# A language model tower on one core: stage ends without the drain of GpSimd's transfer queue

## The reference, cut to what matters

```
h = embedding(x) * 16                        # table of 50000 rows in three parts, a projection each
h = h + four_blocks(layernorm(h))            # per block: q, k, v, a linear attention, gelu, two layer norms, FF 1024
h = h + shared_and_routed_ffn(layernorm(h))  # 8 experts, weights truncated to whole numbers
h = h + attention(layernorm(h))              # 16 heads of 16
h = h + experts64(layernorm(h))              # 64 experts, top 8 of 4 of 8 groups, 256 slots each, and a shared expert
```

## Time and profile before

| | us |
|---|---|
| median of 3 runs | 1364.64 |
| span of the profiled execution, first to last instruction | 1361.2 |
| median less span | 3.4 |
| stage 1 (to 55.5) | 55.5 |
| stage 2 (55.5 to 826.8) | 771.3 |
| stage 3 (826.8 to 925.4) | 98.6 |
| stage 4 (925.4 to 1205.0) | 279.6 |
| stage 5 (1205.0 to 1361.2) | 156.2 |

### The profile page before, as it was taken

The page is one execution under the profiler, slowest core; times in us unless marked ns, Lnnn a source line. Parts: engine busy times, 40 slices in busy tenths (PEclk is TensorE's granted clock), DMA queues, the critical chain, the costliest instruction groups (busy, mean ns, idle before and its releaser), DMA issues. The chain is left out here.

```text
span 1361.2 us, 15556 instructions
## 1 busy us (share of the span) xinstructions
PE 1145.9 (84%) x4506; PEld 634.1 (47%) x4506; DVE 688.7 (51%) x1935; ACT 602.7 (44%) x995; POOL 302.8 (22%) x314
## 2 busy tenths in 40 slices
PE   5649999999999999999999885665987877868872
PEld 4424444444444444444444433441554445446661
DVE  2245645664556455644564513636878854522221
ACT  3335554555455544554455222351674553014431
POOL 5000100000000000000000001107001765427774
PEclk9769999999999999999999896885998878889996
DMA  3200110221012200112011102055743216138997
GB/s 92 95 0 0 43 66 8 74 74 42 4 61 81 73 19 23 66 50 96 9 43 43 43 0 79 1 116 116 123 71 62 102 54 208 63 113 170 181 232 125
DMA packets 56755, 99.57 MB, mean 73 GB/s; under 512 B 10327, under 2 KB 37555, under 8 KB 56440
## 3 DMA queue, kind: packets, MB, share of 16 engines
q1 hardware_dynamic: 37544, 55.94, 15.4%
q0 software_dynamic: 19152, 42.92, 12.2%
HBM read 55.33 MB, written 53.00 MB: 80 GB/s over the span
## 5 line engine op out<-in xcount | busy, mean ns | idle before, releaser
L418 PE MATMUL b_ring<-b_H,b_w 128*128 128x512 f32 x512 | 224.8, 592 | 0.0
L418 PE MATMUL b_ring<-b_X1T,b_w 128*128 128x512 f32 x512 | 223.5, 595 | 0.0
L612 POOL TENSOR_TENSOR b_rstd<-b_veps,b_mhalf 128x4 f32<-128x4 f32 x32 | 32.6, 1019 | 707.0 <-DVE b_veps L69 707.0
L418 PE MATMUL b_ring<-XT,b_wqkv 128*128 128x512 f32 x384 | 174.8, 599 | 7.0 <-DMA b_wqkv<-in_wqkv 7.0
L418 PEld LDWEIGHTS b_ring<-b_X1T,b_w 128*128 128x128 f32 x512 | 96.5, 191 | 116.3 <-issue 109.5
L418 PEld LDWEIGHTS b_ring<-b_H,b_w 128*128 128x128 f32 x512 | 96.1, 190 | 115.2 <-issue 115.2
L568 ACT ACTIVATE b_H<-b_ring,b_cur 128x512 f32<-128x512 f32 x128 | 88.0, 687 | 76.9 <-PE b_ring L418 69.8
L418 PEld LDWEIGHTS b_ring<-XT,b_wqkv 128*128 128x128 f32 x384 | 71.5, 193 | 85.8 <-issue 78.1
L669 DVE RECIPROCAL b_rec<-b_den 128x1024 f32<-128x1024 f32 x16 | 104.9, 6553 | 0.6
L1773 DVE TENSOR_REDUCE a_nmax<-a_pA 128x2 f32<-128x512 f32 x128 | 84.8, 687 | 31.7 <-PE a_pA L1469 29.6
L543 ACT ACTIVATE b_ffo<-b_ring,b_cur 128x512 f32<-128x512 f32 x32 | 22.0, 687 | 170.1 <-PE b_ring L418 170.1
(11 more groups left out here) (309 smaller groups left out, 1799.9 us busy)
## 6 DMA issues: line engine op xcount, KB each, us to landing
xe<-b_nil POOLq DMA_DIRECT2D x16, 1284.0 KB, 5.3
x_rows<-xe SPq DMA_DIRECT2D x32, 321.0 KB, 3.9
b_w<-in_w SPq DMA_DIRECT2D x8, 1024.0 KB, 5.2
x_wt<-in_wexp SPq DMA_DIRECT2D x16, 384.0 KB, 4.4
b_wqkv<-in_wqkv SPq DMA_DIRECT2D x4, 768.0 KB, 4.6
qparts<-f_part SPq DMA_DIRECT2D x8, 384.0 KB, 5.0
right<-qparts SPq DMA_DIRECT2D x16, 192.0 KB, 4.8
left<-qparts SPq DMA_DIRECT2D x16, 192.0 KB, 5.1
```

The lines of the kernel that those rows point to most:

```text
L418: last = pe.matmul(bank[:, :], lhsT(k), rhs(k), start=(k == 0), stop=(k == n_k - 1))
L612: pool.tensor_tensor(rstd[:, :], veps[:, :], mhalf[:, :], ALU.pow).then_inc(s_rs, 1)
```

## The change

In each of the five functions one argument is added:

```
-        block = ctx.enter_context(nc.Block())
+        block = ctx.enter_context(nc.Block(no_gpsimd_drain=True))
```

## The result

| | before | after |
|---|---|---|
| first measurement, median | 1364.83 us (4 runs) | 1355.24 us (1353.56 to 1357.98, 4 runs) |
| ratio, first measurement | | 0.9935, 95% interval 0.9918 to 0.9952 |
| ratio, second to fourth | | 0.9954 (0.9936 to 0.9971), 0.9957 (0.9941 to 0.9972), 0.9956 (0.9943 to 0.9970) |
| all runs of the four measurements, median | 1364.26 us (63 runs) | 1357.83 us (1353.56 to 1359.96, 23 runs) |
| span of the profiled execution | 1361.2 | 1352.0 |

The change makes the kernel 6.4 us faster over all runs, against 5.6 forecast. The first measurement alone gave 8.9 (9.6 between its medians).

A forecast was written before the change was run, and what follows sets the result against it. POOL's queue drains were taken to bound the ends of stages 2 and 5; −2.76 + 0.10 + 0.05 + 0.20 − 3.17 = −5.58 us took 1364.64 to 1359.1 us, 8-in-10 range 1356.9 to 1363.8.

The forecast's parts named there:

- which drains are exposed: POOL's drains at the ends of stages 2 (2.76 us) and 5 (3.17 us) are on the path; the others hidden.
- The line: POOL's drains at stage ends 1, 2 and 4: 0.0815 us per transfer since the last drain, plus 0.07 to 0.09 us.
- second reading of stage 5: Stage 5's last drain, 3.17 us instead of 5.6 for 68 transfers: accumulating transfers have a smaller price each.
- its first: Stage 5's last drain, 3.17 us: about 38 entries' worth was left, the others having been done during the stage.
- the reset drain: Cleanup behind the barriers: 0.10 us more for stage 2's 33 unsettled transfers, 0.05 us for stage 1's 16.
- A: Cleanup drains behind stages 1 and 2 pay 0.0815 us per transfer: −1.7 us, 1362.9; chance 0.13.
- The barrier cost: Semaphore instructions replace the other engines' drains: 0.07 us each at stage ends 1, 3 and 4, 0.2 us together.
- Rival B: The last drain's 3.17 us come back outside the span, at launch closing: −2.4 us, 1362.2; chance 0.10.
- Rival D: Nothing changes, because drains stay in the program under another name: 1364.6; chance 0.04.
- The sum: Terms for the stage ends alone: −2.76 + 0.10 + 0.05 + 0.20 − 3.17 = −5.58 us.
- the clock's term: TensorE's clock return behind stage 2 may shift a little either way: ±1 us in the range, 0 in the sum.
- what lies around it (3.4 us): Time outside the profiled span, taken as 3.4 us and unchanged by the change.

The follow-up runs named there:

- second to fourth: The whole change measured three more times, kernel unchanged, against the kernel before: −6.3 us (8 runs), −5.9 us (6 runs), −6.0 us (5 runs).
- the three parts: Kernel before without GpSimd's drain at one end only: end of stage 2 0.9974, end of the program 0.9978, end of stage 4 1.0005.
- the settling moved: Kernel before, all drains kept, plus a plain POOL drain at the head of each of stage 2's 16 loop turns: 0.9984, −2.2 us.
- fewer transfers: Kernel before, all drains kept, with stage 2 zeroing `odd` in one transfer instead of 16: 1.0003 (0.9992 to 1.0015).

## Why the prediction was right, and where it was wrong

**Right: which drains are exposed.** Ends 2 and 5 gave all of theirs, the end of stage 4 alone gave nothing. Stages 1 and 3 were not run alone; in the trace of after their ends gain nothing.

**Right: the price is bookkeeping for each transfer.** The line was drawn through three drains, and five more lie on it within 0.04 us (3, 4, 18, 20 and 44 transfers; the four joining ones alone took 0.372 us, line 0.41). It holds for transfers that have landed. The prediction's second reading of stage 5, a smaller price for accumulating transfers, was wrong, its first (some were done during the stage) right.

**Right: the reset drain does not settle** (A refuted); I had it at 0.10 us more, it is nothing. The barrier cost 0.06, 0.06 and 0.07 us at stages 1, 3 and 4, where 0.20 was taken for the three. Rival B: 0.1 us and not 3.17. Rival D: the drains are gone.

**Wrong: work outside the ends stood at nothing.** This is the step that failed. The sum has terms for the ends alone and 0 for all the rest, and the range's lower end, 2.2 us below the forecast, leaves little room for it. The prediction itself says: "About 0.2% (2.7 us) is what a measurement of this kernel can tell from no change". It uses this for the line between faster and same, not for the range. In the first profile stage 2 up to ACT's end was 1.1 us shorter and stage 5 up to its first joining transfer 1.6 us, both untouched. Single runs of the changed kernel spread over 6.4 us (1353.56 to 1359.96), those of the kernel before over 10.0. Four of them put the median at 1355.24, and nineteen later ones at 5.9 to 6.3 us below before, inside the range. Of the 8.9 us of the first measurement, the change's own size explains 6.4; the other 2.5 are not shown to have a cause in the change. That four runs happened to lie low is what the repeats leave as an explanation; it is not shown.

One doubt stays open. Stage 5 up to its first joining transfer took 138.3 to 140.6 us in the seven profiles of kernels with all five ends changed, and 139.9 to 141.4 in before and five others that leave this stretch alone (the three parts, the settling moved, fewer transfers). Stage 4's end alone, which hands over the unsettled queue, gave 141.4 in one profile, which speaks against the queue as the cause. Whether the rest is chance is not known.

**Wrong: the clock's term.** "I put ±1 us into the range and 0 into the sum." It is a term of the sum. The four profiles of the changed kernel have a stage 3 of 97.66 us in the mean, against 98.47 in the seven with this end's drain untouched: −0.8 us, with the barrier's 0.06 in it. With it the terms are −2.76 − 0.8 + 0.06 + 0.07 − 3.17 + 0.1 = −6.5 us, against 6.4 measured over all runs and 5.9 to 6.3 in the three later measurements. The size lies within the ±1, so this term alone did not put the result outside the range. The mechanism was wrong: I had read the clock as a small shift around a fixed value; the table shows it to be a step that depends on the gap, −0.8 us at a gap of 2.4 and some +1.5 at one of 3.5 to 3.9. Where the step lies could not have been told from the trace of before. That −0.8 came out and not +1.5 was luck.

**Wrong without effect:** "what lies around it (3.4 us)". It was the median of some runs less the span of another. Where both come from one run it is 1.7 us for this kernel; the difference cancels, as the same 3.4 stood on both sides.

## What to carry to other kernels

A drain at a stage's end costs its time only on the engine that arrives last, so look for the one release that the others wait for, and find what its length counts: here 0.0815 us for each of POOL's transfers since its last drain. Removing it is worth it if what comes behind does not settle in its place; if the drain must stay, put another where POOL waits anyway, or issue fewer and larger transfers. A shift of 1 to 3 us ahead of a stage in which TensorE's clock comes back can be given back whole, or grow by over a quarter, by when it comes back: measure the stage behind as well, before the change is blamed or praised.

## What was not expected of the hardware

- For transfers that have landed, POOL's plain drain depends on their count and nothing else that was seen: 84 transfers took 6.931 us at the end of stage 4 and the same 6.931 us at the start of stage 5. "VectorE: DVE Perf Modes", section "The DRAIN you can't avoid", in the Trainium skill speaks of drains of some 12 ns on all five engines that come from around the kernel. The drains here are the kernel's own: SP's at 7 ns and PE's at 13 ns are of that size, POOL's is up to some 500 times that.
- What is owed has a limit, and it is not the same for all transfers: at least 84 for scatters, 44 to 53 for additions into memory, 38 after four joining transfers.
- A plain drain that meets transfers under way ends 0.12 to 0.13 us after the last has landed (5.1 to 5.7 us with two under way).
- The same stage 3, with nothing in it changed, takes 97.7, 98.5 or 100.0 us with a gap of 2.4, 5.2 or 3.9 us ahead of it.
